# A new order of the engines' steps in a delta-rule attention kernel

## What is computed

```python
q, k, v = x @ Wq, x @ Wk, x @ Wv          # 4 heads, DK = 128, DV = 32
beta = sigmoid(x @ Wb); k = k * rsqrt(sum(k*k) + 1e-12); q = q * SCALE
for t:                                    # delta rule, state S[b, h, DK, DV]
    delta = (v_t - k_t^T S) * beta_t
    S = S + k_t delta^T
    o_t = q_t^T S
o = o * rsqrt(mean(o*o) + 1e-5) * norm_w * silu(x @ Wg)
x = layernorm(x + o @ Wo)
# experts: 8, the top 2 of a softmax, capacity 640 rows for each
x = layernorm(x + sum over experts of p_e * (silu(h @ w1_e) * (h @ w3_e)) @ w2_e)
```

## Time and profile before

| | us |
|---|---|
| median of three runs | 539.06 (538.29 to 539.09) |
| the profiled execution, its own time | 539.08 |
| its span, first to last instruction | 537.2 |
| PE busy, 90% of the span | 484.6 |
| DVE busy, 62% | 332.4 |
| ACT busy, 60% | 324.4 |
| POOL busy, 60% | 324.0 |
| attention, to the last `project` | 7 to 317 |
| experts' products | 332 to 505 |

### The profile page before, as it was taken

The page is one execution under the profiler, slowest core; times in us unless marked ns, Lnnn a source line. Parts: engine busy times, 40 slices in busy tenths (PEclk is TensorE's granted clock), DMA queues, the critical chain, the costliest instruction groups (busy, mean ns, idle before and its releaser), DMA issues.

```text
span 537.2 us, 18867 instructions
## 1 busy us (share of the span) xinstructions
PE 484.6 (90%) x7053; PEld 404.5 (75%) x7053; DVE 332.4 (62%) x1320; ACT 324.4 (60%) x905; POOL 324.0 (60%) x445
## 2 busy tenths in 40 slices
PE   6979989999999999999978977999999999999910
PEld 4665766777677777676755767999999999999910
DVE  4434468758678687686867882555455554555445
ACT  2644666777677777767655742555555555555464
POOL 3052716867758678576886452376677766767652
PEclk9996999999999999999998998999999999999975
DMA  3357575474562655526547134254546545453376
GB/s 94 31 86 215 147 217 53 51 100 76 68 59 28 102 52 68 59 24 109 50 59 147 25 36 109 36 107 56 107 72 115 106 54 105 83 100 34 31 147 196
DMA packets 154164, 45.83 MB, mean 85 GB/s; under 512 B 107040, under 2 KB 148640, under 8 KB 154080
## 3 DMA queue, kind: packets, MB, share of 16 engines
q1 hardware_dynamic: 132208, 29.60, 28.4%
q0 software_dynamic: 20288, 9.51, 18.9%
q10 hardware_dynamic: 1584, 5.59, 2.7%
HBM read 21.13 MB, written 23.55 MB: 83 GB/s over the span
## 4 chain that ended last, share of the span: by engine, by line
PE 73%; DMA 9%; issue 5%; DVE 5%; POOL 2%; ACT 2%; SPq 2%; ACTq 0%; DVEq 0%; POOLq 0%
PE ps L984 17%; PE ps L998 12%; PE ps L722 5%; PE ps L707 4%; PE ps L679 3%; PE ps L682 2%; PE ps L756 2%; PE ps L746 2%; PE ps L848 2%; PE ps L766 2%; PE ps L778 2%; PE ps L736 2%; PE ps L874 2%; PE ps L683 2%; PE ps L684 2%
## 5 line engine op out<-in xcount | busy, mean ns | idle before, releaser
L1753 POOL DMA_INDIRECT x_store<-xk,row x80 | 124.0, 1550 | 68.6 <-ACT xk L1242 46.1
L1712 POOL DMA_INDIRECT slots_in<-x,slot x64 | 99.6, 1556 | 25.9 <-issue 16.2
L1572 DVE TENSOR_TENSOR hb<-ps,hs 128x320 f32<-128x320 f32 (+1 forms) x128 | 62.8, 491 | 53.9 <-ACT hs L1234 52.3
L1234 ACT ACTIVATE hs<-ps 128x320 f32<-128x320 f32 (+1 forms) x128 | 55.8, 436 | 35.6 <-PE ps L984 28.3
L998 PE MATMUL ps<-w2s,hb 128*128 128x128 f32 x640 | 74.1, 275 | 0.0
L998 PEld LDWEIGHTS ps<-w2s,hb 128*128 128x128 f32 x640 | 72.8, 192 | 0.0
L984 PE MATMUL ps<-xeTh,w13h 128*128 128x320 f32 x224 | 71.2, 318 | 1.1 <-DVE xeTl L1596 1.0
L984 PE MATMUL ps<-xeTl,w13h 128*128 128x320 f32 x224 | 69.8, 311 | 0.0
L984 PE MATMUL ps<-xeTh,w13l 128*128 128x320 f32 x224 | 69.7, 311 | 0.0
L1694 POOL TENSOR_TENSOR prod<-a,xs 128x28 f32<-128x28 f32 (+11 forms) x120 | 32.6, 272 | 33.6 <-DVE xs L1407 24.9
L1242 ACT ACTIVATE xk<-ps,gs 128x128 f32<-128x128 f32 x80 | 24.2, 364 | 45.4 <-PE ps L998 45.4
(11 more groups left out here) (208 smaller groups left out, 1082.7 us busy)
## 6 DMA issues: line engine op xcount, KB each, us to landing
slots_in<-zeros ACTq DMA_DIRECT2D x10, 520.0 KB, 5.3
xe<-slots_in SPq DMA_DIRECT2D x15, 325.0 KB
w<-w_in SPq DMA_DIRECT2D x8, 448.0 KB
xTs<-xT SPq DMA_DIRECT2D x4, 512.0 KB, 5.5
a_diag<-hb SPq DMA_DIRECT2D x64, 32.0 KB
inv<-xs SPq DMA_DIRECT2D x16, 128.0 KB
xi<-inv SPq DMA_DIRECT2D x16, 128.0 KB
xk<-x SPq DMA_DIRECT2D x8, 256.0 KB, 6.8
```

The lines of the kernel that those rows point to most:

```text
L1234: af(hs[to, s % 4, :], ps[src, HB[fill_of(s) % 5], 0:HALF], ACT.Silu).then_inc(hs_ready, 1)
L1572: v.tensor_tensor(hb[rows_, par, c, HALF * g:HALF * g + HALF], ps[rows_, at, 0:HALF], hs[rows_, s % 4, :], ALU.mult).then_inc(h_ready, 1)
L1712: g.indirect_dma_start(out=xs_d[:, :], out_offset=bass.IndirectOffsetOnAxis(ap=to, axis=0), in_=x1[:, p % 2, j, k, :], in_offset=None, com ...
L1753: g.indirect_dma_start(out=x1_d[:, :], in_=ye[:, par, i, :], in_offset=None, out_offset=bass.IndirectOffsetOnAxis(ap=row[:, par, i:i + 1], ...
```

## The change

Every engine's loop gets a new order. On TensorE `z_128` of one chunk and `z_32` of the next stand together, so do `w_128` and `w_32`, `deltas`, `state_queries` and `z_64`, and `outputs`, `state_keys` and `w_64`: four runs. `z_128` and `w_128` move to bank CB. Lags grow by one in most places, there is one step more, and rings are longer to match. `count`, `place` and `scatter` go behind by another step; `scaled_values` stands one step later in GpSimd's loop. Some waits follow the new order. The diff without its context lines (in the loops with it) and with less indentation:

```diff
@@ -32,7 +32,7 @@
-XF, XR = 5, 5
+XF, XR = 5, 6
@@ -46,11 +46,11 @@
-STEP_FILLS = (("v", 1, 0), ("kk", 1, 0), ("kq", 5, 1), ("g", 4, 0), ("gq", 4, 0), ("gq", 4, 1), ("kk", 1, 1),
-  ("y", 0, 0), ("kq", 4, 0), ("y", 0, 1))
-LAST = 9
-YR, AR, VR = 4, 4, 4
+STEP_FILLS = (("v", 1, 0), ("kk", 1, 0), ("kk", 1, 1), ("kq", 6, 1), ("g", 5, 0), ("gq", 5, 0), ("gq", 5, 1),
+  ("y", 0, 0), ("y", 0, 1), ("kq", 5, 0))
+LAST = 10
+YR, AR, VR = 5, 5, 4
@@ -300,8 +300,8 @@
-xeTh = sb("xeTh", [P, 2, CAP], F32R)
-xeTl = sb("xeTl", [P, 2, CAP], F32R)
+xeTh = sb("xeTh", [P, 2, XR * P], F32R)
+xeTl = sb("xeTl", [P, 2, XR * P], F32R)
@@ -577,7 +577,7 @@
-    at(store_x1, p - 6)
+    at(store_x1, p - 7)
@@ -728,7 +728,7 @@
-    wait(pe, t128_out, n)
+    wait(pe, t64_out, n)
@@ -771,11 +771,13 @@
+    pe.wait_ge(r_out, n + 1)
-            last = mm(ps[s, LV, 64 * h:64 * h + 64], A[64:128, n % AR, u, 0:64], TT[64:128, u, 64:128],
+            last = mm(ps[s, CB, 64 * h:64 * h + 64], A[64:128, n % AR, u, 0:64], TT[64:128, u, 64:128],
@@ -787,7 +789,7 @@
-            last = mm(ps[s, LV, 256 + 64 * h:256 + 64 * h + 64], x64[s, h, :], z128[s, h, :],
+            last = mm(ps[s, CB, 256 + 64 * h:256 + 64 * h + 64], x64[s, h, :], z128[s, h, :],
@@ -841,7 +843,7 @@
-        pe.wait_ge(acc_read, p)
+        wait(pe, acc_read, p - 1)
@@ -883,11 +885,13 @@
+    pe.wait_ge(zs_out, min(p + 2, NP))
+    wait(pe, acc_read, p)
-    pe.wait_ge(zs_out, p + 1)
@@ -901,40 +905,41 @@
 pe.wait_ge(setup_act, 1)
 for p in range(NP + LAST):
     at(values, p - 1)
-    at(turn_keys, p - 5)
+    if p == 5:
+        keep_on(22)
+    at(z_128, p - 6)
+    at(z_32, p - 5)
     at(key_key, p - 1, 0)
-    at(z_128, p - 5)
-    at(project, p - 6)
-    if p == NP + 5:
-        keep_on(9)
-    at(key_query, p - 5, 1)
-    at(w_128, p - 5)
-    at(gate_in, p - 4)
-    at(queries, p - 4, 0)
-    at(deltas, p - 5)
-    at(state_queries, p - 5)
-    at(queries, p - 4, 1)
-    at(turn_deltas, p - 5)
     at(key_key, p - 1, 1)
     if p == 1:
         setup_rest()
-    at(count, p - 6)
-    if p == NP + 5:
+    at(w_128, p - 6)
+    at(w_32, p - 5)
+    at(project_x, p - 7)
+    at(project, p - 7)
+    if p == NP + 6:
+        keep_on(9)
+    at(key_query, p - 6, 1)
+    at(gate_in, p - 5)
+    at(queries, p - 5, 0)
+    at(deltas, p - 6)
+    at(state_queries, p - 6)
+    at(z_64, p - 5)
+    at(turn_deltas, p - 6)
+    at(queries, p - 5, 1)
+    at(new_state, p - 6)
+    at(outputs, p - 6)
+    at(state_keys, p - 5)
+    at(w_64, p - 5)
+    at(keys, p, 0)
+    at(turn_keys, p - 5)
+    at(count, p - 7)
+    if p == NP + 6:
         keep_on(36)
-    if p == 4:
-        keep_on(22)
-    at(z_32, p - 4)
-    at(outputs, p - 5)
-    at(project_x, p - 5)
-    at(keys, p, 0)
-    at(w_32, p - 4)
-    at(new_state, p - 5)
-    at(key_query, p - 4, 0)
-    at(z_64, p - 4)
-    at(state_keys, p - 4)
-    at(head_sums, p - 5)
     at(keys, p, 1)
-    at(w_64, p - 4)
+    at(head_sums, p - 6)
+    at(key_query, p - 5, 0)
 def turn_tile(par, i):
     at, cols, _ = flipped(i // YT)
@@ -1094,6 +1099,7 @@
+    act.wait_ge(x32_out, n + 1)
@@ -1105,13 +1111,13 @@
-    af(z128[:], ps[:, LV, 0:256].rearrange("p (h c) -> p h c", h=H), ACT.Copy).then_inc(z128_out, 1)
+    af(z128[:], ps[:, CB, 0:256].rearrange("p (h c) -> p h c", h=H), ACT.Copy).then_inc(z128_out, 1)
-                  ps[64 * b:64 * b + 64, LV, 256:512].rearrange("p (h c) -> p h c", h=H), ACT.Copy,
+                  ps[64 * b:64 * b + 64, CB, 256:512].rearrange("p (h c) -> p h c", h=H), ACT.Copy,
@@ -1148,7 +1154,7 @@
-    k = 6 * (p - 6) + i - 2
+    k = 6 * (p - 4) + i - 2
@@ -1171,48 +1177,50 @@
 act.wait_ge(setup_mm, 1)
 af(Mk[:].rearrange("p h d -> p (h d)"), ps[:, LV, :], ACT.Copy).then_inc(setup_act, 1)
 for p in range(NP + LAST):
-    at(key_key_out, p - 3, 0)
-    at(z128_copy, p - 7)
-    at(t128_copy, p - 7)
-    at(x1_rstd, p - 8)
-    at(queries_out, p - 6, 0)
-    at(deltas_out, p - 7)
-    at(gate_out, p - 6)
-    at(deltas_turned, p - 7)
-    at(key_key_out, p - 3, 1)
-    if p == 3:
+    at(values_out, p - 1)
+    at(z128_copy, p - 6)
+    if p - 8 < NP - 1:
+        at(softmax, p - 8)
+    if p >= XF:
+        at(x_high, p)
+    clear(p, 0)
+    at(key_key_out, p - 1, 0)
+    clear(p, 1)
+    at(key_key_out, p - 1, 1)
+    if p == 1:
         act.wait_ge(consts_dve, 1)
         act.wait_ge(setup_mm, 2)
         af(Nq[:].rearrange("p h d -> p (h d)"), ps[:, ZA, :], ACT.Copy, scale=SCALE).then_inc(setup_act, 1)
         act.wait_ge(consts_pool, 1)
-    at(softmax, p - 8)
-    at(gate_sigmoid, p - 6)
-    at(key_norms, p - 5)
-    clear(p, 0)
-    at(queries_out, p - 6, 1)
-    if p == 6:
+    at(t128_copy, p - 6)
+    at(x64_diag, p - 5)
+    clear(p, 2)
+    at(gate_out, p - 5)
+    at(queries_out, p - 5, 0)
+    at(deltas_out, p - 6)
+    at(x1_rstd, p - 7)
+    if p - 7 == NP - 1:
+        softmax(NP - 1)
+    at(deltas_turned, p - 6)
+    if p == 4:
         act.wait_ge(setup_act, 2)
         weights_high()
-    clear(p, 1)
-    at(outputs_out, p - 7)
-    at(t_diag, p - 6)
-    clear(p, 2)
-    if p - 7 == NP - 1:
+    clear(p, 3)
+    at(queries_out, p - 5, 1)
+    at(gate_sigmoid, p - 5)
+    at(outputs_out, p - 6)
+    clear(p, 4)
+    if p - 6 == NP - 1:
         w_high(0, 0, 0)
-    at(head_norms, p - 7)
-    if p - 7 == NP - 1:
+    at(key_norms, p - 3)
+    at(t_diag, p - 5)
+    at(keys_out, p, 0)
+    at(keys_out, p, 1)
+    clear(p, 5)
+    at(head_norms, p - 6)
+    if p - 6 == NP - 1:
         w_high(0, 0, 1)
-    at(keys_out, p - 2, 0)
-    clear(p, 3)
-    at(keys_out, p - 2, 1)
-    at(x64_diag, p - 6)
-    clear(p, 4)
-    at(values_out, p - 2)
-    if p > XF:
-        at(x_high, p - 1)
-    clear(p, 5)
 def turn_first():
     for k in (0, 1):
@@ -1525,42 +1533,43 @@
 prepare()
 for p in range(NP + LAST):
+    at(masked, p - 6, 0)
+    at(z32_copy, p - 5)
+    at(x64_turned, p - 6)
+    if p - 8 < NP - 1:
+        at(place, p - 8)
     at(x32_copy, p - 5)
-    at(state_copy, p - 6)
-    at(masked, p - 5, 0)
-    at(z64_copy, p - 5)
-    at(keys_read, p - 5)
-    at(gated_values, p - 6)
-    at(t64_copy, p - 5)
-    if p - 6 == NP - 1:
-        w_low(0, 0, 0)
-    at(gated_out, p - 6)
-    if p - 6 == NP - 1:
-        w_low(0, 0, 1)
-    at(x64_turned, p - 5)
-    at(residues, p - 5)
+    at_group(scale_blocks, p - 2)
+    if p == 2:
+        solve_first()
     if p == XF:
         weights_low()
     if p >= XF:
         at(x_rest, p)
-    at_group(scale_blocks, p - 2)
-    if p == 2:
-        solve_first()
-    at(normalise, p - 6)
-    at(masked, p - 5, 1)
-    at(experts, p - 6)
-    at(inverse_in, p - 4)
-    at(offsets, p - 6)
-    if p - 6 == NP - 1:
+    at(normalise, p - 7)
+    at(masked, p - 6, 1)
+    at(experts, p - 7)
+    at(z64_copy, p - 5)
+    at(state_copy, p - 6)
+    at(offsets, p - 7)
+    if p - 7 == NP - 1:
         x1_out(NP - 1, (0,))
         place(NP - 1)
         x1_out(NP - 1, (1,))
         continue
-    at(x1_out, p - 6)
-    at(z32_copy, p - 4)
-    at(place, p - 6)
+    at(x1_out, p - 7)
+    at(keys_read, p - 5)
+    at(t64_copy, p - 5)
+    at(residues, p - 5)
+    at(gated_values, p - 6)
+    if p - 6 == NP - 1:
+        w_low(0, 0, 0)
+    at(inverse_in, p - 4)
+    at(gated_out, p - 6)
+    if p - 6 == NP - 1:
+        w_low(0, 0, 1)
 def gated(n, par, s):
     dve.wait_ge(hs_ready, 8 * n + s + 1)
@@ -1735,10 +1744,10 @@
         at_group(solve, p)
     if p == 1:
         pool.wait_ge(solved, 1)
-    if p > 1:
-        at(scaled_values, p - 1)
-    at(silu_of, p - 2)
-    at(scatter, p - 4)
+    if p > 2:
+        at(scaled_values, p - 2)
+    at(silu_of, p - 3)
+    at(scatter, p - 6)
 for k in range(2):
     pool.wait_ge(x1_st[k], 16 * (NP // 2))
```

## The result

The changed kernel takes 574.97 us (median of four runs, 573.14 to 576.13), the kernel before in the same comparison 538.67 (537.82 to 539.09): recorded ratio 1.072, interval 1.067 to 1.078 (the two medians by themselves divide to 1.067; the ratios below are the recorded ones). Slower, as forecast, but by 36 us and not by 4; 543.5 us and the range up to 550 miss it.

A forecast was written before the change was run, and what follows sets the result against it. TensorE's instruction order and kind were taken to set attention's pace. Forms -10.6, start +8.4, steady +1, drain +1, end +4.1, its clock +1 gave +4.9, less 0.5 is +4.4: 543.5 us from 539.06, range 533 to 550.

The forecast's parts named there:

- end, with its clock: After attention: place(14) behind gated_out(15) delays the last scatter and experts' load, +4.1 us; likely half clock, +1.
- the rest: Taken off the sum: 0.5 us, for a wait of 0.2 or so that even the shortest old step holds.
- The forms: TensorE's small-product runs: fewer form changes save 0.66 us a chunk (bounds 0.46 and 0.84), 10.6 us over sixteen chunks.
- my sum: Form saving per chunk on TensorE, reckoned by runs: 3 x 0.28 - 2 x 0.09 = 0.66 us.
- The start: First chunks: keys(4) waits for xT, z_32(0) at about 50.3, z_128(0) at 62.3; +8.4 us (bounds +4 and +13).
- V's ring: At the start, values_out(5) needs scaled_values(1), now behind solve on GpSimd; ScalarE is held until 68.
- a term of 3.1: At the start: w_128(0) starts 3.1 us late, as z128_copy(0) stands behind ScalarE's hold.
- The steady part: Nine steps: 16.3 and 17.5 us alternate, mean 16.9; new waits 0.6 a step against 0.5; +1 us (bounds -4, +9).
- The drain: Last chunks: new waits for x64_turned and the scatter against old waits gone; +1 us (bounds -4, +5).
- 12 in four: Drain: new waits of 12 us in four steps, against some 10 us of old waits in three.
- the queues fall behind: Rival, chance 0.12: ScalarE and VectorE pass lateness on, 2 us more each second step, start at high bound; about 553.
- The slow clock lasts: Rival, chance 0.10: filler and small products behind it at half clock at the start, 5 us more, 548 in all.

The follow-up runs named there:

- the three mends: Changed kernel with scaled_values and scatter ahead of solve on GpSimd, load of xT's second quarter, place(14) and softmax(14) a step earlier: 543.43 us, 1.023.
- the split: Against the three mends, z_32 put between the halves of key_key and w_32 behind project, six runs instead of four: 556.54 us, 1.044.
- GpSimd's order alone: Changed kernel with one edit: scaled_values and scatter stand ahead of solve on GpSimd instead of behind it: 558.25 us, 1.037.
- the early `place`: Changed kernel with one edit: place(14) and softmax(14) in step 21, ahead of the last chunk's gated_out: 572.93 us, 1.063.
- all mends: The three mends plus six filler products in steps 17 to 21 and x64_turned between inverse_in and gated_out; the last run: 536.32 us, 1.013.
- the best versions: The three mends with six fillers in steps 17 to 21 (538.39 us, 1.012), and that with x64_turned between inverse_in and gated_out (536.32 us, 1.013).
- the early load: Changed kernel with one edit: SyncE loads xT's second quarter in its step 2 instead of 3: 573.59 us, 1.062.
- all five edits and twelve fillers: Changed kernel with GpSimd's order, early load, early place(14) and softmax(14), x64_turned between inverse_in and gated_out, twelve fillers in steps 17 to 21: 555.82 us, 1.031.

## Why the prediction was wrong

By the profiles, forecast and measured difference to before (the saved changes of form, 0.66 a chunk, put where the chunks are):

| stretch | forecast | measured |
|---|---|---|
| up to `z_128(1)` | 8.4 - 1.3 = +7.1 | +16.9 |
| nine chunks | 1 - 5.9 = -4.9 | 0.0 |
| five chunks, to the last `project` | 1 - 3.3 = -2.3 | +15.4 |
| end, with its clock | +5.1 | +3.7 |
| the rest | -0.5 | +0.4 |

*The forms* held, a little smaller than forecast. TensorE's busy time in nine steps is 153.34 us before and 148.44 with the three mends: 0.54 a chunk, within the bounds of 0.46 and 0.84. The shortest steps, 16.92 and 16.30, differ by 0.62. In the change as made, waits and gaps ate all of it: 158.21 against 158.23. By the rule of the Trainium skill (TensorEngine Tiling (Array Packing), Key Properties) as I applied it (changes of form count, an estimate of 0.54 a chunk) the saving is the 0.54 of the busy time, by my sum it is near the 0.62 of the steps, so the two are not told apart; and the split (two runs more, two changes of form more) cost 0.58 a step of busy time, more than either makes of it. The 7.1 us by which the nine chunks are shorter than before in the table are not all form: the chips differ, and waits are among them.

*The start* was right up to `z_128(0)`, and in the mechanism: V's ring, Vk behind a solve, `w_128(0)` 3.98 us late. Two sizes failed. The clock was at half from 69.3 to 76.1 behind that wait, which I did not count; with `scaled_values` ahead of solve (alone or with scatter) both are gone, 6.8 us for a term of 3.1. And of the 11 us at `z_128(0)` I took off 5, for work done ahead and for waits that the old order had here too; with Vk in time 11.3 us are still 10.0 at `z_128(1)`. The sum has a slip besides: 8 + 3.1 - 2 is 9.1, and 8.4 only with the chunk's 0.7 taken off, which the saving of all sixteen chunks takes off again.

*The steady part*: I followed one pair of steps through the queues and found `x1_out` waiting for the scatter, `turn_keys` 0.8 us late and `w_128` 0.4, mean 16.9. It is 17.58, 6.1 us more over nine steps. This mechanism hardly showed there: TensorE waited once for `turn_keys`, 0.31 us, and twice for `z128_copy`, 0.76 in all. What it waited for instead is `x64_turned`, 2.3 us in two waits, and the gaps of the last section, 3.6 us, for which the sum had no term. ScalarE did wait for Vk, four times and up to 2.7 us, and `x1_out` for the scatter made `turn_keys` late only from step 16 on. GpSimd's order alone takes these waits away, and 3.8 us; gaps stay.

*The drain* is the step that failed most, 17.7 us. I reckoned it wait by wait, "12 in four" steps against 10 of old ones, though the waits that I named come to 9.3. But `w_128` waited 13.4 us for `x64_turned` and not 5.6; in step 19 `z32_copy`, ahead of it on VectorE, is held 1.44 us by TensorE's `z_32`; the clock was at half for 34 us in all, for which the sum had nothing; and the scatter's wait in step 16 (1.7 us), with half clock from there on, started the chain late. Mending GpSimd's order gives 8.8 us of it back, though it touches neither `x64_turned` nor the clock directly: the waits for `x64_turned` fall to 9.0 us and half clock to 14. That this is because the later engines then start in time is argued from the trace, not shown by a run of its own.

*The end* was right in its cause, +3.7 for 4.1 and 1; the early `place` gives 2.5 of it back, and with all mends it is 13.96 against 13.40.

Of the rivals "the queues fall behind" names what happened, at the low chance of 0.12 and 22 us short. Its price, 8 to 13 us, was made of steady steps and a start at its high bound of +13, with nothing for the drain; the lateness costs most at the start and in the drain, where no work of other chunks covers it. "The slow clock lasts" was looked for in the wrong place: the clock was up again at 45.3 us, just ahead of the filler, and fell later, behind the waits of `turn_keys` and `w_128`.

The sign was right for a reason that held, the start and the end, which lost 20.6 us by themselves; but the drain, where the sum saw a gain of 2.3, lost 15.4.

Open stays why the best versions are still 1.2 and 1.3 per cent above. In the profile of the last the first chunk comes 7.8 us later, against a whole difference of 7.0 us on its chip; I put that down to the step added to the pipeline, but no run took that step back alone.

## What to carry to other kernels

When a step is put into a pipeline, follow each strict queue's longest block (here 12 us of solve) and ask of everything behind it who waits for it now that it is one step closer; do this for the first and the last chunks by themselves, for there nothing covers it. When a single mend of a late chain brings little, look in the mended trace for where the gain went: the early load had step 7 start 6.9 us sooner and the last `project` 2.2, with the scatter's wait grown to 3.34 us in step 18. Then mend that, and measure the first mends again; whether they are worth more then is not shown here. An order of a queue is right for one place of its inputs only: by the ratios, scatter ahead of solve was worth some 10 us with Vk before it, cost 24 without, and 85 in the old order. And compare kernels of one chip, or busy time: here the chips were as far apart as the mends.

## What the runs showed of the hardware

TensorE stands still inside joined runs of small products with no wait of the program. In nine steps of the changed kernel there are nine such gaps of 0.24 to 0.50 us, 3.6 in all; measured between the starts of neighbouring products, 0.41 to 0.68 us, it is 5.2. In the same steps of the kernel before no two neighbours in a run start more than 0.17 apart. Two of them, by TensorE's timeline, and one of 2.08 us in the kernel with three mends:
```profile
141.96 0.58 PE L746 MATMUL ps<-z,xi 32*32 32x16 f32 x37 [0.26 <-issue]
...
147.52 0.55 PE L756 MATMUL ps<-x32T,hb 32*32 32x32 f32 x11 [0.46 <-issue]
```
```profile
277.47 0.46 PE L746 MATMUL ps<-z,xi 32*32 32x16 f32 x31
...
280.01 0.63 PE L746 MATMUL ps<-z,xi 32*32 32x16 f32 x33 [2.08 <-issue]
```
The profile's transfers of 277 to 281 us hold one of the instruction queue:
```profile
q8 instruction: 1, 0.02, 1.4%
```
The Trainium skill, Runtime: NRT & Kernel Launch, Instruction fetch mechanics, has instructions fetched in blocks by a queue of their own, mostly hidden. These gaps could be the part that is not, when 80 small products follow each other and the transfer comes late. No run shows it, and the trace speaks as much against it: for three of the nine gaps (those that end at 120.45, 182.84 and 227.75 us) there is no transfer of the instruction queue in the 3 us before. What the profiles, one for each kernel, do show is that the gaps go with the chip. All kernels with joined runs that ran on the first three chips have them, those on the last three hardly any in these steps (one, of 0.36 us; in the drain three have one of over 2 us): the same nine steps have 17 gaps without a semaphore's wait, 7.8 us, with all five edits and twelve fillers, and none with six fillers on another chip. The kernel before was profiled on the first chip only, so that longer runs are needed for them is not shown either.
